# A Strassen layer's weight sums and its residual plus bias: made on GpSimd in SBUF, or by accumulating transfers in DRAM

## What is computed

```python
def _sage_layer(h, edge_src, edge_dst, deg_inv, W_self, W_neigh, b):
    msg = h[edge_src]
    agg = jax.ops.segment_sum(msg, edge_dst, num_segments=h.shape[0])
    mean = agg * deg_inv[:, None]
    return h @ W_self + mean @ W_neigh + b
h = jax.nn.relu(_sage_layer(layernorm(x), ..., W_self0, W_neigh0, b0))
x = x + _sage_layer(h, ..., W_self1, W_neigh1, b1)
```

## Time and profile before

| | |
|---|---|
| median of 3 runs | 1112.87 us (1103.74 to 1113.25) |
| the profiled execution's own time | 1110.37 us |
| its span, first to last instruction | 1108.6 us |
| mean granted TensorE clock | 0.979 |

### The profile page before, as it was taken

How to read it: one execution, slowest core, us unless ns; L and a number is a source line. 1 busy time by engine, 2 the same in 40 slices (tenths; PEclk the granted TensorE clock), 3 DMA queues, 4 the chain that set the end, 5 groups by cost and what they waited for, 6 DMA issues and landing times.

```text
span 1108.6 us, 17295 instructions
## 1 busy us (share of the span) xinstructions
PE 1048.8 (95%) x5765; PEld 929.2 (84%) x5765; DVE 732.3 (66%) x1192; ACT 467.3 (42%) x1042; POOL 331.6 (30%) x285
## 2 busy tenths in 40 slices
PE   5999999999999998989998999999999989999995
PEld 4999999999999996767686777889999679999994
DVE  6678888888752338988538789553221468878883
ACT  5555434453311222435203334454332257777772
POOL 5500000000000226656506683002442124554532
PEclk9999999999999999999998999999999889999998
DMA  7332133213227772333135422465565087999971
GB/s 190 95 106 71 44 107 108 73 46 99 71 71 217 204 208 64 112 138 114 49 111 150 143 85 68 138 198 160 154 182 190 20 310 237 318 307 288 307 219 30
DMA packets 76803, 160.80 MB, mean 145 GB/s; under 512 B 13315, under 2 KB 38141, under 8 KB 72221
## 3 DMA queue, kind: packets, MB, share of 16 engines
q1 hardware_dynamic: 65053, 128.42, 36.2%
q0 software_dynamic: 10976, 30.74, 10.7%
q10 hardware_dynamic: 672, 0.32, 0.1%
HBM read 124.32 MB, written 42.96 MB: 151 GB/s over the span
## 4 chain that ended last, share of the span: by engine, by line
PE 74%; DVE 9%; issue 7%; POOL 3%; DMA 3%; ACT 2%; DVEq 1%; SPq 0%; POOLq 0%; ACTq 0%
PE ps L1065 14%; PE ps L1717 10%; PE ps L2364 9%; PE ps L1679 8%; PE ps L1377 7%; PE ps L2385 6%; PE ps L1664 5%; PE ps L910 4%; PE ps L824 3%; PE ps L2350 2%; POOL bw_lo L1299 2%; POOL bw_sum L1285 1%; ACT hs_hi L1361 1%; DVE hs_sum L1334 1%; DVE hs_sum L1342 1%
## 5 line engine op out<-in xcount | busy, mean ns | idle before, releaser
L1285 POOL TENSOR_TENSOR bw_sum<-bw_sum,bw_raw 128x512 f32<-128x512 f32 x40 | 60.9, 1533 | 337.4 <-DMA bw_raw<-in_L_gnn_W_self 294.9
L1664 PE MATMUL ps<-bw_hi,hs_hi 128*125 128x512 f32 x280 | 114.9, 410 | 19.4 <-POOL bw_lo L1299 10.8
L917 DVE TENSOR_TENSOR adj<-ps,adj 125x250 f32 x212 | 88.1, 416 | 41.6 <-PE ps L910 33.5
L1664 PE MATMUL ps<-bw_hi,hs_lo 128*125 128x512 f32 x280 | 112.4, 402 | 0.0
L1664 PE MATMUL ps<-bw_lo,hs_hi 128*125 128x512 f32 x280 | 112.4, 401 | 0.0
L1065 PE MATMUL ps<-h_lo,w_hi 128*128 128x418 f32 x336 | 108.5, 371 | 0.0
L1299 POOL TENSOR_TENSOR bw_lo<-bw_sum,bw_hi 128x512 fp32r<-128x512 f32 x56 | 83.4, 1495 | 81.0 <-ACT bw_hi L1293 81.0
L1065 PE MATMUL ps<-h_hi,w_hi 128*128 128x418 f32 x336 | 100.3, 379 | 0.0
L2458 DVE TENSOR_TENSOR w_lo<-w_raw,w_hi 128x2048 fp32r<-128x2048 f32 x34 | 77.8, 2289 | 25.6 <-ACT w_hi L2413 22.1
L1065 PE MATMUL ps<-h_hi,w_lo 128*128 128x418 f32 x336 | 93.4, 359 | 0.0
L1377 PE MATMUL ps<-adj,y_hi 125*128 125x416 f32 (+1 forms) x240 | 85.9, 358 | 1.7 <-DMA self<-self_d 1.2
(11 more groups left out here) (306 smaller groups left out, 2679.8 us busy)
## 6 DMA issues: line engine op xcount, KB each, us to landing
w_raw<-in_L_ffn_ew SPq DMA_DIRECT2D x34, 1024.0 KB, 7.9
bw_sum<-in_L_gnn_W_neigh SPq DMA_DIRECT2D x20, 512.0 KB, 5.7
bw_raw<-in_L_gnn_W_self SPq DMA_DIRECT2D x16, 512.0 KB, 4.8
xin<-in_x SPq DMA_DIRECT2D x10, 448.0 KB
t_d<-xn SPq DMA_DIRECT2D x10, 448.0 KB
base<-x_d POOLq DMA_DIRECT2D x10, 448.0 KB, 4.4
out<-base POOLq DMA_DIRECT2D x10, 448.0 KB, 3.4
y_d<-y_hi SPq DMA_DIRECT2D x7, 625.0 KB
```

Source lines behind the costliest of these rows:

```text
L917: e.tensor_tensor(cols, ps[0:P, 5 + b % 2, 0:KW].rearrange("p (t w) -> p t w", t=NT), cols, ALU.add).then_inc(self.took, 1)
L1285: e.tensor_tensor(own, own, bw_raw[:, k, :], ALU.subtract if FORM(g) in (3, 4) else ALU.add).then_inc(bw_s, 1)
L1664: mm = e.matmul(ps[0:P, bank, :], ht[slot_of(n)][:, k, :], wt[u][:, k, :], start=(form not in ONTO and k == 0 and i == 0), stop=(k == KH - ...
```

## The change

- The sum of the two blocks is no longer made in SBUF, except for form 1 (one group in each half). For the four other summed forms, in both halves, POOL issues during layer 0 a DRAM-to-DRAM copy of the first block into `sum_d` (eight of 512x512, 1.05 MB each) and later an accumulating transfer of the second block onto it. In the same way `xb_d` (5.12 MB) gets the bias of each of the 1250 rows and then `x` added. POOL issues the nine plain transfers behind its clearing of `adj`, waits for all, and issues the nine accumulating ones.
- `block_load` reads those groups from `sum_d`, `residual_load` reads `xb_d`. SP waits for all 18 transfers (`s_sums`) just before `block_load(e, 0)`.
- Gone are `with_bias`, `bias_load`, the semaphore `s_x` (now `s_in`), 32 of the 40 `block_sum` and 16 of the 20 `raw_load` transfers.
- Signs: blocks that were subtracted are now added, the node sums of forms 1, 2 and 5 become differences to match. The count of node instructions is the same.
- `block_low` is two instructions of 256 columns instead of one of 512; PE waits for both.

```diff
-SUMMED_B = (1, 3, 4, 6, 7)
+SUMMED_B = (1,)
+ADDED = (3, 4, 6, 7)
+NADD = NQ * len(ADDED)
@@
+        xb_d = nc.dram_tensor("xb_d", (N, D), F32, kind="Internal").ap()
+        sum_d = nc.dram_tensor("sum_d", (NADD, D // 2, HALF), F32, kind="Internal").ap()
@@ (gpsimd, behind the last memsets of adj)
+            added = [(q, i, form) for q in range(NQ) for i, form in enumerate(ADDED)]
+            for q, i, form in added:
+                e.dma_start(sum_d[len(ADDED) * q + i], weight_block(q, form, 0)).then_inc(s_sums, 16)
+            e.dma_start(xb_d, I["L0_gnn_b1"].partition_broadcast(N)).then_inc(s_sums, 16)
+            e.wait_ge(s_sums, 16 * (NADD + 1))
+            for q, i, form in added:
+                e.dma_start(sum_d[len(ADDED) * q + i], weight_block(q, form, 1), accum_op=ALU.add).then_inc(s_sums, 16)
+            e.dma_start(xb_d, I["x"], accum_op=ALU.add, max_dma_last_dim=4 * D).then_inc(s_sums, 16)
@@ half_block
+            if i == 0 and form in ADDED:
+                rows = sum_d[len(ADDED) * q + ADDED.index(form)]
@@ block_low
-            e.tensor_tensor(bw_lo[u][:, k, :], bw_sum[u][:, k, :], bw_hi[u][:, k, :].bitcast(F32), ALU.subtract).then_inc(bw_l, 1)
+            for a in range(0, HALF, HALF // 2):
+                cols = slice(a, a + HALF // 2)
+                e.tensor_tensor(bw_lo[u][:, k, cols], bw_sum[u][:, k, cols], bw_hi[u][:, k, cols].bitcast(F32),
+                                ALU.subtract).then_inc(bw_l, 1)
@@ nodes_sum
-                    ins = e.tensor_tensor(to, low_rows(p), high_rows(p + PAIRS), ALU.add)
+                    ins = e.tensor_tensor(to, low_rows(p), high_rows(p + PAIRS), ALU.subtract)
@@ sync, aggregation of layer 0
                 if i == 1:
                     e.wait_ge(x_full, 3 * KT)
                     e.wait_ge(z_full, 3 * KT + 3)
+                    e.wait_ge(s_sums, 32 * (NADD + 1))
                     block_load(e, 0)
-                    raw_load(e, 0)
@@ gpsimd, layer 1
-            prepare(0)
-            prepare(1)
-            with_bias(0)
-            for g in range(2, MS + 2):
-                prepare(g)
-            with_bias(1)
-            for g in range(MS + 2, NQ * MS):
+            for g in range(NQ * MS):
                 prepare(g)
@@ tensor, unit
-                        e.wait_ge(bw_l, KH * g + k + 1)
+                        e.wait_ge(bw_l, 2 * (KH * g + k + 1))
```

More of the change, by code:

```diff
@@ L307, in build @@
         L = Region(R_CONST + 3072)
-        b1_at = L.at
-        b1t = L("b1t", [P, HALF], F32)
-        row_at = [R_SLAB + 8192, L.at, b1_at]
+        row_at = [R_SLAB + 8192, L.at, L.at + 4 * HALF]
         L = Region(R_ACC)
@@ L652, in slab_high, with weight_block @@
             e.activation(w_hi[:, u, :, :], w_raw[:, u, :, :], ACT.Copy).then_inc(done, 1)
+        N1_W = (I["L0_gnn_W_neigh1"], I["L0_gnn_W_self1"])
+        BLOCKS_OF = {1: ((0, 0), (1, 1)), 2: ((0, 0), None), 3: ((1, 0), (1, 1)), 4: ((0, 1), (0, 0)),
+                     5: ((1, 1), None), 6: ((0, 0), (1, 0)), 7: ((0, 1), (1, 1))}
+        def weight_block(q, form, i):
+            v, low_half = BLOCKS_OF[form][i]
+            return N1_W[v][D // 2 * low_half:D // 2 * (low_half + 1), HALF * q:HALF * (q + 1)]
         @on("gpsimd")
@@ L1246, in build @@
         s_st = [sem(f"s_st{g}") for g in range(3)]
-        N1_W = (I["L0_gnn_W_neigh1"], I["L0_gnn_W_self1"])
         nat = lambda a: a.rearrange("(t p) n -> p t n", p=P)
-        x_view, x2_view = nat(I["x"]), nat(x2_d)
+        xb_view, x2_view = nat(xb_d), nat(x2_d)
         tile_of = lambda i: slice(i * P, (i + 1) * P)
         group_of = lambda i: min(i // 4, 2)
-        BLOCKS_OF = {1: ((0, 0), (1, 1)), 2: ((0, 0), None), 3: ((1, 0), (1, 1)), 4: ((0, 1), (0, 0)),
-                     5: ((1, 1), None), 6: ((0, 0), (1, 0)), 7: ((0, 1), (1, 1))}
         def half_block(g, i, k):
-            v, low_half = BLOCKS_OF[FORM(g)][i]
-            a = HALF * (g // MS)
-            return view(N1_W[v])[:, KH * low_half + 2 * k:KH * low_half + 2 * k + 2, a:a + HALF]
+            q, form = g // MS, FORM(g)
+            if i == 0 and form in ADDED:
+                rows = sum_d[len(ADDED) * q + ADDED.index(form)]
+            else:
+                rows = weight_block(q, form, i)
+            return view(rows)[:, 2 * k:2 * k + 2, :]
         def block_load(e, g):
@@ L1284, in block_sum @@
                 e.wait_ge(raw_in[k // 2], 16 * sums_b_to(g) + 16)
-                e.tensor_tensor(own, own, bw_raw[:, k, :], ALU.subtract if FORM(g) in (3, 4) else ALU.add).then_inc(bw_s, 1)
+                e.tensor_tensor(own, own, bw_raw[:, k, :], ALU.subtract).then_inc(bw_s, 1)
         def block_high(e, g, k):
@@ L1414, in _ @@
                 residual_load(e, 0, g)
-            raw_load(e, 2)
             for g in range(2, MS + 1):
@@ L1535, in _ @@
             residual_next(2)
-            raw_load(e, MS + 2)
             for g in range(MS + 2, NQ * MS):
@@ L1922, in taken @@
                 if form == 3:
-                    e.wait_ge(s_x, 3 * q + 1 + p // 4)
+                    e.wait_ge(s_in[p // 4], 32 * q + 32)
                     onto(own)
                 if form == 6:
-                    e.wait_ge(s_x, 3 * q + 2 + (p + PAIRS) // 8)
+                    e.wait_ge(s_in[1 + (p + PAIRS) // 8], 32 * q + 32)
                     onto(other)
```

26 lines of the change are left out of this document (4 added, 22 removed).

## The result

| | before | after |
|---|---|---|
| median of 4 runs each, measured side by side | 1111.17 us (1103.74 to 1113.25) | 1146.78 us (1140.60 to 1150.44) |
| the profiled execution's own time | 1110.37 us | 1150.44 us |
| its span | 1108.6 us | 1148.7 us |
| mean granted TensorE clock | 0.979 | 0.959 |

The changed kernel is slower: ratio 1.033, 95% interval 1.026 to 1.040. Forecast were 1129 us and 19 us of loss; 35.6 us were measured by the medians, 40.1 by the profiled executions. Layer 1 gave what was expected, layer 0 lost half as much again. The time lies within the stated range, near its upper end of 1150.

A forecast was written before the change was run, and what follows sets the result against it. TensorE, busy 95% of the span, was taken as the bound, so time is won only where it idles or its clock falls. 1110.4 - 21 (layer 1) + 40 (layer 0) = 1129 us; range 1089 to 1150, likeliest case 1115 to 1150.

The forecast's parts named there:

- Direction and mechanism: Slower, 0.46: in layer 0 new traffic delays the W_neigh0 slab load, ACT waits, TensorE stalls; layer 0 loses 40 us.
- how much later the load lands: Layer 0's W_neigh0 slab load, 15.6 us before, lands 9.4 us later during copies and 12 during accumulations.
- the worst case: Upper end for the layer 0 slab load: +22 us, a full turn for every turn at 2.4 times dearer accumulation.
- The stalls that follow from it: TensorE stalls in four layer 0 slabs hit before 227 us: 9 + 10 + 10 + 5 = 34 us.
- The allowances of 0.3 and 2 us: Load delay in layer 0 tolerated before TensorE stalls: 0.3 us in the first slab, 2 in the others.
- The clock's 6 us: Four falls of TensorE's clock after layer 0's stalls, at 1.65 us each, cost 6 us more.
- The traffic's own sum: New DRAM traffic in layer 0: copies 36 us and accumulations 90 us of all 16 engines, 126, ending about 227 us.
- SP's wait at nothing: SP's added wait for the sums, wanted at 336.9 us, costs nothing, with 110 us of cover.
- Layer 1's 21 us: Layer 1 gains 21 us, 14 to 26, from removed bias addition, removed sums and halved low parts.
- Its split: Layer 1's gain: 13.6 us for the bias addition gone, 8 for 32 of 40 sums gone and low parts halved.
- hidden-traffic rival: Layer 0 loads land at most 2 us later, loss 0 to 9 us, time 1089 to 1099; chance 0.32.
- late sums: Transfers issued so slowly they run past 336.9 us; SP then stops TensorE, time above 1200; chance 0.03.

The follow-up runs named there:

- the wide rows: Changed kernel with layer 0's W_neigh0 slab loaded as 128 rows of 4 KB instead of 1024 pieces of 512 B: 1127.0 us, ratio 1.016.
- the early load and the spread stores together: Changed kernel with the next W_neigh0 load issued once its buffer is free, and y_hi0 and y_lo0 stored as 112 and 13 rows: 1087.4 us, ratio 0.982.
- the early load: Changed kernel with the next W_neigh0 slab load issued as soon as its buffer is free, not behind the stores: 1113.1 us, ratio 1.006.
- the spread stores alone: Changed kernel with only the y_hi0 and y_lo0 stores cut into 112 and 13 rows: median 1111.2 us over 11 runs, from 1105.9 to 1139.7.

## Why the prediction was right or wrong

**Direction and mechanism: right.** The place (next `W_neigh0` slab), the chain (ACT waits, no chunk keys, TensorE waits for `adj`), the start of the traffic at 53.4 us and the clock under 1 came as written.

**The step that failed: how much later the load lands.** The prediction took the experts' loads' ratio of 1.6 for this one: 9.4 us with copies, 12 with accumulation. Measured were 29.2, 21.1 and 11.7. Those loads bring 1 MB in 128 rows of 8 KB. This one is 64 small rows for an engine behind up to 58 others, and each takes a turn. That the number of its rows counts is shown by the wide rows, that those ahead count by the early load and the spread stores together. The prediction named the worst case (+22, "a full turn for every turn") and kept it as a bound. Even that was too low for the first slab. It is 1.4 x 15.6, which puts the foreign turn in the place of the load's own; the load's own turn and a foreign one of 2.4 would have been +37.

"A full turn for every turn" should have been priced as pieces ahead of the last byte, times the time of one foreign piece. An estimate with the pieces' mean times in the changed kernel's trace: on a busiest engine 50 store rows of 0.20 us, each with a copy of 0.20, 8 of `self_d` of 0.19 with 0.30, 64 of the slab of 0.045 with 0.30 make 46 us from the first store's issue; measured 113.35 - 66.42 = 46.9. With accumulating pieces of 0.18: 50 x 0.39 + 8 x 0.39 + 64 x 0.22 = 37 us; measured 170.92 - 133.05 = 37.9. It is not the whole price: the early load's first landing, with nothing ahead, would by it be 64 x 0.24 = 15 us and was 84.06 - 62.16 = 21.9, and the spread stores alone stay above it too.

**The stalls that follow from it.** 9, 10, 10 and 5 us were forecast, 30.0, 19.0 and 9.7 measured: 59 against 34. With slabs this long only three met the traffic, not four. The allowances of 0.3 and 2 us held to about 1 us: extensions of 29.2, 21.1 and 11.7 less stalls of 30.0, 19.0 and 9.7 leave -0.8, 2.1 and 2.0. That the first stall is longest, the prediction had the wrong way round: it took accumulation as the slower neighbour.

**The clock's 6 us: right,** about 5. TensorE was busy for 110.3 us in the three slabs, with no more work than in the 105.6 of the same three before. Two of them before (the third is in the earlier trace rows), then the changed kernel behind its first and its third stall:

```profile
67.00:102.00 35.00, 34.95 (x214) 32.49 (x213) 29.82 (x69) 17.05 (x78) 0.00 (x0) 1.00 0.28 88
138.00:174.00 36.00, 35.32 (x216) 32.88 (x215) 29.69 (x69) 15.96 (x75) 0.00 (x0) 1.00 0.27 83
...
114.00:120.00 6.00, 3.86 (x13) 3.65 (x14) 4.55 (x9) 4.50 (x26) 4.61 (x8) 0.50 0.57 87
120.00:126.00 6.00, 6.00 (x34) 5.51 (x33) 4.01 (x9) 0.90 (x5) 3.77 (x4) 0.82 1.09 193
...
218.00:224.00 6.00, 3.47 (x12) 3.27 (x13) 4.56 (x9) 4.62 (x25) 0.00 (x0) 0.50 0.02 4
```

TensorE comes out of each stall at a granted clock of 0.50, the lower level. In the rows of whole slabs (0.74, 0.85, 0.89) most of the low clock is that of idle time, which costs nothing.

**The traffic's own sum was good.** 126 us of 16 engines: the software queue's share rose from 10.7% of 1108.6 us to 20.9% of 1148.7, by 121 us. It was over at about 212 us, not 227. Its parts were not: the copies took 48 us of the 16 engines and not 36, about 22 of them for the bias row (48 less the 26 that the blocks took beside `x`), and the accumulating transfers 73 and not 90.

**SP's wait at nothing: right,** by 188 us of cover: the first load behind it is issued at 399.8, as the aggregation comes to it.

**Layer 1's 21 us: right,** measured 21 by the medians and 23 by the ratio, within 14 to 26; the traces of the units say 26 to 28. A half piece of 0.74 against 0.72, waits on `bw_lo` 4.6 against 3.3, the clock back at 1.00: right. Its split (13.6 for the bias, 8 for the sums) was too much for the bias, 7 to 8, and for the sums 8 by the ratio or 17 by the traces.

**The sum with what was measured.** The changed kernel's first and last low-part weight load, to set beside the kernel before's 419.5 to 694.0:

```profile
L1656 PEld LDWEIGHTS ps<-bw_lo,hs_hi x280: 184/185/189, 479.5 to 726.3; 128*125 128x125 f32 x140
```

The units begin 60.0 us later (forecast 40), last 27.7 us less (forecast 21), and the stretch behind them is 7.8 us longer (forecast 0): 1110.4 + 60.0 - 27.7 + 7.8 = 1150.5, measured 1150.4. The last term is of the kind that follows no edit, and stays open. So the error of the layer-0 step, 20 us, and that term were in part made up for by a layer 1 that gave more. The hidden-traffic rival fell on the landing times; "late sums" fell on the 212 us.

The Trainium skill bears on this in two places that the prediction did not use. The page DMA: Bandwidth & Descriptors of the Trainium skill, "Queues, rings and completion order", says that an engine goes round its queues packet by packet, several descriptors to one. That there are turns, the equal counts (580 and 580) agree with; how many rows make one turn no run here shows, since packets of several rows, as many on one side as on the other, would give the same counts. "Why a DMA increments its semaphore by 16 and not by 1", on the same page of the Trainium skill, says that a transfer is split over the largest number of engines, up to 16, that divides its row count: 5 for 125 rows, as the work for 4.8 engines above agrees with. Cutting 125 into 112 and 13 took about 30 us off the median.

## What to carry to other kernels

Before adding background traffic, list each transfer that an engine waits for while it runs, and count the pieces that it and everything ahead of it in its queue put on the busiest DMA engine: each may wait for one foreign piece, so the latency grows with the count and not with the bytes. Then move those transfers to the earliest point that their buffer allows and spread them, and price the background work again: here the same traffic cost about 60 us in one order and 3 to 7 in another. Such a count tells where the wait is, and its price to within some microseconds at best. Cutting an engine's instructions finer frees its neighbour, but the engine itself gets slower; here, on a POOL without time to spare, the time stayed the same.

## What the runs showed of the hardware

- Under full background traffic a 0.5 MB load of 512 B rows took 44.8 us instead of 15.6; as 4 KB rows 30.7.
- With rows of two queues waiting on every DMA engine, equal numbers of rows ran: 580 of 4 KB and 580 of 512 B in 12 us.
- Copying one 4 KB row of DRAM to 1250 rows took about 22 us of the 16 engines, copying 1250 different rows of 4 KB (as 640 pieces of 8000 B) 14.
- An accumulating piece of 2 KB, DRAM to DRAM, took 0.18 us, one of 4000 B 0.33, a plain one of 4 KB 0.20.
- POOL's addition of a bias row to 1250 rows of 512 columns takes 12.2 us in 3 pieces and 19.7 in 20.
- With the DMA engines full (share 0.96) TensorE was busy for 38.00 of 38 us at full clock.
